# TensorE's slot in another order: output transposes joined with the xn2 transposes, router product next to the h transposes

## The chip, the cores and the metric

The kernel runs on one core of a Trainium2 chip. The metric is the device time of one execution in microseconds (us), lower is better. Engines are called TensorE (PE), VectorE (DVE), ScalarE (ACT), GpSimd (POOL) and SyncE (SP), as the profile's short names have them; PEld is the loading of weights into TensorE.

## The reference

For 32 rows (batch elements) of 512 tokens with 256 channels:

```python
mod = (_silu(L0_c) @ L0_wmod).reshape(32, 6, 1, -1)
sa, ca, ga, sb, cb, gb = ...
h = _layernorm(x, axis=-1) * (1 + ca) + sa
x = x + ga * attn(h)
h = _layernorm(x, axis=-1) * (1 + cb) + sb
x = x + gb * ffn(h)
```

`attn` is a decaying running mean over the tokens (s = a * s + (1 - a) * x_t) times a matrix W, plus a convolution over five tokens per channel. `ffn` has a router: the last token of the row goes through Wp1, gelu and Wp2 to eight logits, and the expert with the largest one is taken for the whole row. The expert is gelu(h W1 + b1) W2 + b2, then Wo, and the result is h + 0.3 * out.

## The kernel before, in words

A row is one unit of work, held whole in the on-chip memory as 128 partitions by 4 tiles of 256 channels (token layout), or as 2 chunks of 128 channels by 512 tokens (channel layout). TensorE changes from one layout to the other by transposes of 128x128, 8 for a row. Products with exact enough results are made from three matmuls each: every operand is split into a high and a low part (`hid_hi`, `hid_lo` and so on), and high x high, low x high and high x low are added up. Setup multiplies W2 and Wo of each expert together, so that only an up product (256 to 512 channels, four groups f = 0 to 3 of six matmuls) and a down product (512 to 256, again four groups of six) are left.

The rows go through a software pipeline with slots i = -3 to 32. In slot i the feed-forward part of row i is computed, row i - 1 is finished and stored, row i + 1 is normalised the second time and routed, row i + 2 goes through mix (W) and convolution, and row i + 3 is normalised the first time and scanned. Each engine has its own list of instructions in program order, written by hand as a function `slot(i)` per engine; they meet only at semaphores. Nothing is scheduled by a tool. TensorE's slot is the subject (`slot`, line 978). Before the change it is in this order:

- `mix(i + 2)` (L915, L916, L919; twelve matmuls, which need S_hi and S_lo of the row)
- the output transposes (`to_tokens(Q, rT, t4_done)`, L967 into the banks Q), after a wait for `oT_ready`
- `up(i, 0)`, `up(i, 1)` (L935 to L937)
- the xn2 transposes ("t3", `to_channels`, L975 into the banks TR)
- `down(i, 0)` (L950, L951 with g_hi, L955 with g_lo), then the first half of `up(i, 2)`
- the router's first product (L1005, four matmul instructions of one column), after waits for `hid_ready` and `gelu_out`
- the second half of `up(i, 2)`
- the h transposes of row i + 3 ("t1", L975 into TR)
- the router's second product (L1017, L1018), after a wait for `nav_ready`
- `down(i, 1)`, `up(i, 3)`, the transposes of the first residual ("t2", L967 into TR), `down(i, 2)`, `down(i, 3)`

ScalarE's slot (L570) is in this order: normalise xn1 (row i + 3) and xn (row i + 1), L507; gelu and g_hi of f = 0 and 1 (L547, L554); hid (L613) and hid_hi (L621) of row i + 1; the router's gelu `nav` (L630), which waits for `r_nav`, the semaphore of the router's first product; `gate1` (L567); gelu 2; h (L643); g_hi 2; S_hi, gelu 3, g_hi 3, S_hi (L541); hid_gated (L679).

GpSimd's slot (L440): the second normalisation's factors; g_lo 0 and 1 (`g_low`, L430, each after a wait for its g_hi); gbeta; hid_lo; the first normalisation's factors (L413 to L418); g_lo 2 and 3; S_lo 0 (L438).

VectorE's slot (L779): rT of row i - 1 (L787); the first `CONV_HEAD` = 4 of ten convolution steps (L748); the two additions of the transposed output to xr (L798), which set `o_ready`; the other steps; statistics (L700); the router's maximum (L829, L831), which sets `sel_ready`; two scans (L776), which wait for h; the first residual with its statistics and S_lo 1 (L764, L755). The banks Q are also where down accumulates, so `down(i, 0)` waits for `o_ready`.

SyncE's queue issues all DMAs of the loop, in program order: the two stores of row i - 1 after `o_ready` (L386), the load of x of row i + 5 into the same buffer once they have landed (L297), and then `fetch(i + 1)` (L362): after `sel_ready` it reads the number of the expert and loads up_w (L375) and down_w (L378). `up(i, 0)` waits for up_w, `down(i, 0)` for down_w.

Of the kernel before, what the change touches and what calls it, by code (L numbers as in the profile page):

```python
# [5 lines left out]
def adaln_attention_ffn_kernel(nc, x, decay_logit, W, b, conv_w, conv_b, Wp1, bp1, Wp2, bp2,  # L6
# [26 lines left out]
    DC = D // P  # L33
# [31 lines left out]
    with ExitStack() as ctx:  # L65
# [6 lines left out]
        def sem(name):  # L72
            return ctx.enter_context(nc.semaphore(name))
# [172 lines left out]
        up_done = sem("up_done")  # L246
# [10 lines left out]

        VECS_LOADED = 16 * 7
        SMALL_LOADED = 16 * 4
        CONV_HEAD = 4  # L260
        CONV_MID = 7
        FIRST = -3

# [7 lines left out]
        def experts_at(i, place):  # L271
            return EXPERTS_AT.get((i, place), ())

        def wait(eng, s, v):
            if v > 0:
                eng.wait_ge(s, v)

        def row(r):
            return 0 <= r < B
# [406 lines left out]
        def _(dve):  # L686
# [55 lines left out]
            def conv(r, first, last):  # L742
                for k, c in CONV_ORDER[first:last]:
                    if k == 0:
                        dve.wait_ge(mix_done, DC * r + c + 1)
                    else:
                        dve.wait_ge(conv_step[c], (TAPS - 1) * r + k)
                    ins = nc.vector.scalar_tensor_tensor(out=Y[c][:, :], in0=h[:, c, k:k + T], scalar=taps[:, c, k:k + 1],  # L748
                                                         in1=Y[c][:, :], op0=ALU.mult, op1=ALU.add)
                    ins.then_inc(conv_step[c] if k < TAPS - 1 else conv_done, 1)  # L750
# [28 lines left out]
            def slot(i):  # L779
# [9 lines left out]
                if row(i + 2):  # L789
                    if i == -2:  # L790
                        dve.wait_ge(s_small, SMALL_LOADED)
                    conv(i + 2, 0, CONV_HEAD)
                if row(i - 1):
# [6 lines left out]
                if row(i + 2):  # L800
                    conv(i + 2, CONV_HEAD, CONV_MID)
                mix_experts = experts_at(i, "mix")
# [41 lines left out]
        def _(pe):  # L844
            mm = nc.tensor.matmul

            def w2_transposes(e):
                pe.wait_ge(s_w2[W2_AT[e]], 16 * nth(W2_AT, e))
                wait(pe, s_w2T, DC * e)
                for c in range(DC):  # L850
                    for f in range(FC):
                        ins = nc.tensor.transpose(U[c][:, f * P:(f + 1) * P], w2_nat(e)[:, f, c * P:(c + 1) * P], ident[:, :])
                ins.then_inc(s_w2T_mm, 1)
# [3 lines left out]
            for c in range(DC):  # L857
                ins = nc.tensor.transpose(U[0][:, c * B:(c + 1) * B], c_nat[:, c * P:(c + 1) * P], ident[0:B, 0:B])
# [5 lines left out]
            for n in range(NMOD):  # L864
                pe.wait_ge(s_wmod[n], 16 * DC)
                for c in range(DC):
                    ins = mm((Y[0], Y[1], Q[0])[n][0:B, :], silu_cT[:, c], wmod_sb[c][n], start=(c == 0), stop=(c == DC - 1))
                ins.then_inc(s_mod_mm, 1)
            w2_transposes(0)
            for m in range(6 * DC):  # L870
                n, at = m * P // 512, m * P % 512
                pe.wait_ge(s_mod_rows, n + 1)
                ins = nc.tensor.transpose(Q[1][:, m * B:(m + 1) * B], mod_rows[n][:, at:at + P], ident[0:B, 0:B])
            ins.then_inc(s_modT, 1)
            pe.wait_ge(s_w, 16)
            for d in range(DC):
                for e in range(DC):
                    ins = nc.tensor.transpose(Y[0][:, d * D + e * P:d * D + (e + 1) * P], w_nat[:, e, d * P:(d + 1) * P], ident[:, :])
# [10 lines left out]
            def expert(e):  # L889
                if e + 1 < E:  # L890
                    w2_transposes(e + 1)
                pe.wait_ge(s_w2T, DC * (e + 1))
                for k in range(2):
                    if e == 0:

                        pe.wait_ge(s_mod_rows, NMOD)
                        pe.wait_ge(s_mods, 1)
                    wait(pe, s_down_lo, 2 * (e - 1) + k + 1 if e else 0)
                    for f in range(FC // 2):
                        fk = k * FC // 2 + f  # L900
                        for c in range(DC):
                            ins = mm(Q[k][:, f * D:(f + 1) * D], w2T(e)[:, c, fk * P:(fk + 1) * P], wo[:, c],
                                     start=(c == 0), stop=(c == DC - 1))
                    ins.then_inc(s_comb, 1)
# [14 lines left out]
                        ins = mm(Y[e][:, :], mix_w[:, 0, d, es], S_lo[:, d], start=False, stop=(d == DC - 1))  # L919
                    ins.then_inc(mix_done, 1)  # L920

            def up(i, f, parts=range(DC)):
                par, n = i % 2, FC * i + f
                if f == 0:
                    pe.wait_ge(up_loaded[par], 16 * (i // 2 + 1))
                    pe.wait_ge(hid_lo_ready, DC * (i + 1))
                if f == 1:
                    wait(pe, sel_ready, i + 1)
                if f == 3:

                    pe.wait_ge(sel_ready, min(i + 2, B))
                wait(pe, gelu_out, n - 1)
                for c in parts:
                    w = c * F + f * P
                    mm(U[f % 2][:, :], up_w[:, par, UP + w:UP + w + P], hid_hi[:, par, c], start=(c == 0), stop=False)  # L935
                    mm(U[f % 2][:, :], up_w[:, par, w:w + P], hid_hi[:, par, c], start=False, stop=False)  # L936
                    ins = mm(U[f % 2][:, :], up_w[:, par, w:w + P], hid_lo[:, par, c], start=False, stop=(c == DC - 1))  # L937
                if DC - 1 in parts:
                    ins.then_inc(up_done, 1)

            def down(i, f):
                par, n = i % 2, FC * i + f
                if f == 0:
                    pe.wait_ge(down_loaded[par], 16 * (i // 2 + 1))

                    wait(pe, o_ready, HB * i)
                pe.wait_ge(g_hi_ready, n + 1)
                for c in range(DC):
                    w = f * D + c * P
                    mm(Q[c][:, :], down_w[:, par, 1, w:w + P], g_hi[:, f], start=(f == 0), stop=False)  # L950
                    mm(Q[c][:, :], down_w[:, par, 0, w:w + P], g_hi[:, f], start=False, stop=False)  # L951
                pe.wait_ge(g_lo_ready, n + 1)
                for c in range(DC):
                    w = f * D + c * P
                    ins = mm(Q[c][:, :], down_w[:, par, 0, w:w + P], g_lo[:, f], start=False, stop=(f == FC - 1))  # L955
                    if f == FC - 1:
                        ins.then_inc(down_done, 1)
                if f < FC - 1:
                    ins.then_inc(down_step, 1)
# [18 lines left out]
            def slot(i):  # L978
                if row(i + 2):
                    mix(i + 2)  # L980
                for e in experts_at(i, "mix"):
                    expert(e)
                if row(i - 1):
                    pe.wait_ge(oT_ready, DC * i)
                    to_tokens(Q, rT, t4_done)
                if row(i):
                    up(i, 0)
                    up(i, 1)
                if row(i + 1):
                    to_channels(i + 1, xn, xn2_ready, t3_done)  # L990
                for e in experts_at(i, "t3"):
                    expert(e)
                if row(i):
                    down(i, 0)
                    up(i, 2, (0,))
                if row(i + 1):
                    r = i + 1
                    if r == 0:
                        pe.wait_ge(s_small, SMALL_LOADED)
                    pe.wait_ge(hid_ready, DC * (r + 1))  # L1000

                    wait(pe, gelu_out, FC * i + 2 if i >= 0 else 0)
                    pe.wait_ge(s_w2T, DC * E)
                    for c in range(DC):
                        ins = mm(U[1][:, 0:1], wp1[:, c], hid_at[r % 2][:, c, T - 1:T], start=(c == 0), stop=(c == DC - 1))  # L1005
                    ins.then_inc(r_nav, 1)
                if row(i):
                    up(i, 2, (1,))
                if row(i + 3):
                    r = i + 3  # L1010
                    to_channels(r, xn1, xn1_ready, t1_done)
                    if r == 0:
                        betas()
                if row(i + 1):
                    r = i + 1
                    pe.wait_ge(nav_ready, r + 1)
                    mm(U[1][0:1, 8:8 + E], nav[:, :], wp2[:, :], start=True, stop=False)  # L1017
                    mm(U[1][0:1, 8:8 + E], ident[0:1, 0:1], bp2_sb[:, :], start=False, stop=True).then_inc(r_logits, 1)  # L1018
                for e in experts_at(i, "t1"):
                    expert(e)  # L1020
                if row(i):
                    down(i, 1)
                    up(i, 3)
                if row(i + 2):
                    r = i + 2

                    pe.wait_ge(h_ready, DC * min(r + 2, B))
                    pe.wait_ge(r1_ready, DC * (r + 1))
                    to_tokens(TR, rT, t2_done)
                if row(i):  # L1030
                    down(i, 2)
                    down(i, 3)
# [31 lines left out]
```

## Time and profile before

| what | value |
|---|---|
| median of 3 runs | 693.33 us (693.09 to 694.68) |
| the profiled execution's own time | 696.09 us |
| its span | 694.1 us |
| TensorE busy | 661.3 us, 95% (3431 matmuls) |
| weight loads busy | 523.1 us, 75% |
| VectorE busy | 570.2 us, 82% |
| ScalarE busy | 570.6 us, 82% |
| GpSimd busy | 459.3 us, 66% |
| granted TensorE clock, mean | 0.974 |

The profile shows one execution. "Busy" is the time in which an engine had an instruction in work; matmuls overlap each other, so that a matmul of 0.39 us may be followed by the next after 0.23 us, and it is the distance of the starts that counts. The granted clock is 1 at 2.4 GHz and 0.5 at 1.2 GHz. Times in a timeline are counted from the start of the span.

### The profile page before, as it was taken

How to read it: one execution, taken by the hardware profiler on the slowest of the kernel's cores; microseconds unless marked ns; L12 is line 12 of the kernel's file. 1: busy time of each engine (PE TensorE's matmuls, PEld its weight loads, DVE VectorE, ACT ScalarE, POOL GpSimd, SP SyncE). 2: the span in 40 equal slices, each digit the busy share in tenths (PEclk: the TensorE clock that was granted, in tenths of full speed). 3: DMA queues.
4: the chain of work that ended last, by engine and by line, in shares of the span. 5: the costliest groups of instructions: out<-in, count | busy, mean ns of one | idle time of the engine just before them, and what ended most of it. 6: DMA issues, size and time to landing. Idle time of an engine off the chain costs nothing.

```text
span 694.1 us, 11042 instructions
## 1 busy us (share of the span) xinstructions
PE 661.3 (95%) x3431; PEld 523.1 (75%) x3431; DVE 570.2 (82%) x870; ACT 570.6 (82%) x979; POOL 459.3 (66%) x528
## 2 busy tenths in 40 slices
PE   5969679999999999999999999999999999999996
PEld 2858557777777878777777777787877778777764
DVE  1677649999999999999999999999999999998711
ACT  3676658888888998888888888899898888887753
POOL 1453537777777777777777777777777777776543
PEclk9798969999999999999999999999999999999998
DMA  7995645555655444555555555545455545544451
GB/s 231 328 301 171 224 153 159 175 171 165 183 182 167 170 131 159 169 179 169 167 181 163 173 181 182 156 149 157 163 167 182 176 160 182 157 148 153 151 170 44
DMA packets 55453, 120.57 MB, mean 174 GB/s; under 512 B 5643, under 2 KB 43364, under 8 KB 46180
## 3 DMA queue, kind: packets, MB, share of 16 engines
q1 hardware_dynamic: 51316, 115.12, 52.7%
q10 hardware_dynamic: 4080, 4.75, 2.5%
q8 instruction: 28, 0.46, 0.3%
q14 instruction: 29, 0.24, 0.1%
HBM read 61.12 MB, written 25.19 MB: 124 GB/s over the span
## 4 chain that ended last, share of the span: by engine, by line
PE 85%; DMA 2%; ACT 2%; POOL 2%; issue 1%; DVE 0%; POOLq 0%; SPq 0%; DVEq 0%; ACTq 0%
PE Q L955 9%; PE Q L950 9%; PE U L935 9%; PE U L937 9%; PE U L936 8%; PE Q L951 8%; PE TR L975 8%; PE Y L919 5%; PE Q L967 4%; PE Y L915 4%; PE Y L916 4%; PE TR L967 4%; PE U L1005 2%; DMA up_table<-up_w 1%; DMA up_w<-up_table 1%
## 5 line engine op out<-in xcount | busy, mean ns | idle before, releaser
L430 POOL TENSOR_TENSOR g_lo<-g,g_hi 128x512 fp32r<-128x512 f32 x128 | 191.3, 1503 | 144.2 <-ACT g_hi L554 138.9
L748 DVE SCALAR_TENSOR_TENSOR Y<-h,taps,Y 128x512 f32<-128x512 f32 x320 | 222.7, 751 | 3.1 <-PE Y L919 0.7
L935 PE MATMUL U<-hid_hi,up_w 128*128 128x512 f32 x256 | 107.1, 418 | 4.7 <-DMA up_w<-up_table 4.7
L950 PE MATMUL Q<-g_hi,down_w 128*128 128x512 f32 x256 | 109.8, 429 | 0.2
L547 ACT ACTIVATE g<-U,up_w 128x512 f32<-128x512 f32 x128 | 88.6, 692 | 25.4 <-PE U L937 22.5
L507 ACT ACTIVATE S<-xr,nmr,rstd 128x256 f32<-128x256 f32 x128 | 66.6, 592 | 48.0 <-POOL S_lo L438 36.4
L937 PE MATMUL U<-hid_lo,up_w 128*128 128x512 f32 x256 | 101.6, 397 | 0.0
L936 PE MATMUL U<-hid_hi,up_w 128*128 128x512 f32 x256 | 101.6, 397 | 0.0
L951 PE MATMUL Q<-g_hi,down_w 128*128 128x512 f32 x256 | 101.1, 395 | 0.0
L776 DVE TENSOR_TENSOR_SCAN S<-keep,h 128x512 f32<-128x512 f32 x64 | 78.0, 1261 | 26.0 <-ACT h L643 26.0
L700 DVE BATCH_NORM_STATS2 st<-xr 128x6 f32<-128x512 f32 x128 | 87.6, 705 | 7.9 <-DMA xr<-in_L_attn_x_dram 3.6
L955 PE MATMUL Q<-g_lo,down_w 128*128 128x512 f32 x256 | 83.7, 408 | 0.7 <-POOL g_lo L430 0.7
L554 ACT CAST g_hi<-g 128x512 fp32r<-128x512 f32 x128 | 80.5, 629 | 3.1
L507 ACT ACTIVATE xn<-xr,nmr,rstd 128x256 f32<-128x256 f32 x128 | 66.5, 591 | 9.5 <-POOL nmr L418 7.2
L416 POOL TENSOR_TENSOR rstd<-rstd,minus_half 128x4 f32<-128x4 f32 x64 | 66.5, 1039 | 0.0
L955 PEld LDWEIGHTS Q<-g_lo,down_w 128*128 128x128 f32 x256 | 45.0, 187 | 23.7 <-POOL g_lo L430 14.4
L787 DVE SCALAR_TENSOR_TENSOR rT<-Q,mods,w_raw 128x512 f32<-128x512 f32 x64 | 44.6, 739 | 18.0 <-PE Q L955 18.0
L935 PEld LDWEIGHTS U<-hid_hi,up_w 128*128 128x128 f32 x256 | 48.8, 191 | 14.1 <-DMA up_w<-up_table 5.4
L937 PEld LDWEIGHTS U<-hid_lo,up_w 128*128 128x128 f32 x256 | 48.6, 190 | 11.4
L438 POOL TENSOR_TENSOR S_lo<-S,S_hi 128x512 fp32r<-128x512 f32 x32 | 54.5, 1704 | 1.9 <-ACT S_hi L541 1.9
L950 PEld LDWEIGHTS Q<-g_hi,down_w 128*128 128x128 f32 x256 | 48.2, 188 | 10.0 <-ACT g_hi L554 0.9
L936 PEld LDWEIGHTS U<-hid_hi,up_w 128*128 128x128 f32 x256 | 49.0, 191 | 8.8
(125 smaller groups left out, 1283.3 us busy)
## 6 DMA issues: line engine op xcount, KB each, us to landing
up_w<-up_table SPq DMA_DIRECT2D x32, 1027.0 KB, 6.6
down_w<-down_tab SPq DMA_DIRECT2D x32, 1024.0 KB, 8.6
xr<-in_L_attn_x_dram SPq DMA_DIRECT2D x32, 512.0 KB, 3.6
out_dram<-xr SPq DMA_DIRECT2D x64, 256.0 KB, 2.3
w_raw<-in_L_ffn_W_dram SPq DMA_DIRECT2D x7, 512.0 KB, 5.2
xr<-in_L_ffn_W_dram ACTq DMA_DIRECT2D x6, 512.0 KB, 7.9
up_table<-down_w SPq DMA_DIRECT2D x2, 1024.0 KB, 7.1
up_table<-up_w SPq DMA_DIRECT2D x2, 1024.0 KB, 6.0
```

Source lines behind the costliest of these rows:

```text
L430: nc.gpsimd.tensor_tensor(g_lo[:, f], g[:, f % 2], g_hi[:, f].bitcast(f32), ALU.subtract).then_inc(g_lo_ready, 1)
L507: nc.scalar.activation(to[:, j], xr[:, r % NX, j], ACT.Identity, bias=nmr[:, j:j + 1], scale=rstd[:, j:j + 1]).then_inc(ready, 1)
L547: nc.scalar.activation(g[:, f % 2], U[f % 2][:, :], ACT.Gelu, bias=up_w[:, i % 2, U_B1 + f:U_B1 + f + 1].bitcast(f32)).then_inc(gelu_out, 1)
L554: nc.scalar.copy(g_hi[:, f], g[:, f % 2]).then_inc(g_hi_ready, 1)
L700: return nc.vector.bn_stats(st[:, k * TPB:(k + 1) * TPB].rearrange("p t s -> p (t s)"), pair)
L748: ins = nc.vector.scalar_tensor_tensor(out=Y[c][:, :], in0=h[:, c, k:k + T], scalar=taps[:, c, k:k + 1], in1=Y[c][:, :], op0=ALU.mult, op1 ...
L935: mm(U[f % 2][:, :], up_w[:, par, UP + w:UP + w + P], hid_hi[:, par, c], start=(c == 0), stop=False)
L936: mm(U[f % 2][:, :], up_w[:, par, w:w + P], hid_hi[:, par, c], start=False, stop=False)
L937: ins = mm(U[f % 2][:, :], up_w[:, par, w:w + P], hid_lo[:, par, c], start=False, stop=(c == DC - 1))
L950: mm(Q[c][:, :], down_w[:, par, 1, w:w + P], g_hi[:, f], start=(f == 0), stop=False)
L951: mm(Q[c][:, :], down_w[:, par, 0, w:w + P], g_hi[:, f], start=False, stop=False)
L955: ins = mm(Q[c][:, :], down_w[:, par, 0, w:w + P], g_lo[:, f], start=False, stop=(f == FC - 1))
```

## The change

TensorE's list is put into another order, and one constant of VectorE's list changes with it.

- The output transposes go from in front of `up(i, 0)` to behind `up(i, 1)`, directly ahead of the xn2 transposes: sixteen transposes in one piece.
- `up(i, 2)` is no longer split. It comes whole, behind the transposes and ahead of `down(i, 0)`.
- The router's first product comes behind `down(i, 0)`, directly ahead of the h transposes.
- `CONV_HEAD` goes from 4 to 6: on VectorE the two output additions come behind six convolution steps.

The lists of ScalarE, GpSimd and SyncE are the same.

```diff
-        CONV_HEAD = 4
+        CONV_HEAD = 6
...
-            def up(i, f, parts=range(DC)):
+            def up(i, f):
...
-                for c in parts:
+                for c in range(DC):
...
-                if DC - 1 in parts:
-                    ins.then_inc(up_done, 1)
+                ins.then_inc(up_done, 1)
...
+                if row(i):
+                    up(i, 0)
+                    up(i, 1)
                 if row(i - 1):
                     pe.wait_ge(oT_ready, DC * i)
                     to_tokens(Q, rT, t4_done)
-                if row(i):
-                    up(i, 0)
-                    up(i, 1)
                 if row(i + 1):
                     to_channels(i + 1, xn, xn2_ready, t3_done)
                 for e in experts_at(i, "t3"):
                     expert(e)
                 if row(i):
+                    up(i, 2)
                     down(i, 0)
-                    up(i, 2, (0,))
                 if row(i + 1):
...
                     ins.then_inc(r_nav, 1)
-                if row(i):
-                    up(i, 2, (1,))
                 if row(i + 3):
                     r = i + 3
                     to_channels(r, xn1, xn1_ready, t1_done)
```

## Rows read from the trace of the kernel before

**Rows 1.** Windows: length, busy us (instructions) of each engine, granted clock, DMA share, GB/s.

```profile
109.00:688.70 579.70, 574.75 (x3028) 454.91 (x3028) 505.19 (x764) 504.32 (x865) 411.65 (x473) 1.00 0.52 164
...
93.60:98.10 4.50, 4.43 (x11) 3.47 (x11) 2.06 (x4) 1.31 (x2) 0.05 (x1) 0.50 0.61 233
```

**Rows 2.** Line 1005, the router's first product: count, ns min/median/max, first and last start.

```profile
L1005 PE MATMUL U<-w_raw,wp x60: 239/250/253, 101.6 to 629.1; 128*128 128x1 f32 x60
...
L1005 PE MATMUL U<-hid,wp x56: 247/250/262, 120.4 to 610.3; 128*128 128x1 f32 x56
```

**Rows 3.** Timeline of TensorE, slot 12: start us, us from first start to last end.

```profile
320.91 1.03 PE L967 MATMUL Q<-ident,rT 128*128 128x128 f32 x8
321.70 0.48 PE L935 MATMUL U<-hid_hi,up_w 128*128 128x512 f32 x1
322.02 0.39 PE L936 MATMUL U<-hid_hi,up_w 128*128 128x512 f32 x1
...
322.94 0.40 PE L937 MATMUL U<-hid_lo,up_w 128*128 128x512 f32 x1
...
327.54 0.58 PE L1005 MATMUL U<-w_raw,wp 128*128 128x1 f32 x4
327.98 0.48 PE L935 MATMUL U<-hid_hi,up_w 128*128 128x512 f32 x1
328.30 0.39 PE L936 MATMUL U<-hid_hi,up_w 128*128 128x512 f32 x1
...
334.44 0.40 PE L951 MATMUL Q<-g_hi,down_w 128*128 128x512 f32 x1
334.83 0.74 PE L955 MATMUL Q<-g_lo,down_w 128*128 128x512 f32 x2
```

**Rows 4.** Timeline of ScalarE, slot 12, and its window 328.38 to 332.41.

```profile
323.37 0.69 ACT L547 ACTIVATE g<-U,up_w 128x512 f32<-128x512 f32 x1 [0.18 <-PE U L937]
...
327.35 1.13 ACT L621 CAST hid_hi<-w_raw 128x512 fp32r<-128x512 f32 x2
328.38 0.26 ACT L630 ACTIVATE nav<-U,vecs 128x1 f32<-128x1 f32 x1
...
328.38:332.41 4.03, 4.03 (x25) 3.19 (x24) 2.76 (x7) 4.03 (x8) 3.79 (x6) 1.00 0.59 147
```

**Rows 5.** Timeline of GpSimd in slot 12, then g_hi 2 and g_lo 2 in slot 28.

```profile
332.56 3.47 POOL L430 TENSOR_TENSOR g_lo<-g,g_hi 128x512 fp32r<-128x512 f32 x2
...
334.74 1.29 POOL L430 TENSOR_TENSOR g_lo<-g,g_hi 128x512 fp32r<-128x512 f32 x1
...
633.01 0.65 ACT L554 CAST g_hi<-g 128x512 fp32r<-128x512 f32 x1
...
633.80 3.46 POOL L430 TENSOR_TENSOR g_lo<-g,g_hi 128x512 fp32r<-128x512 f32 x2 [1.93 <-ACT g_hi L554]
```

**Rows 6.** VectorE's convolution and SyncE's DMA issues in slot 12; the loads' landing times.

```profile
324.28 4.18 DVE L748 SCALAR_TENSOR_TENSOR Y<-h,taps,Y 128x512 f32<-128x512 f32 x6
...
327.34 0.38 SPq L297 DMA_DIRECT2D xr<-in_L_attn_x_dram  x1
331.36 0.37 SPq L375 DMA_DIRECT2D up_w<-up_table  x1
...
DMA to landing us min/median/max: 5.3/6.6/6.9
...
xr<-in_L_attn_x_dram SPq DMA_DIRECT2D x32, 512.0 KB, 3.6
```

**Rows 7.** Timeline of slots 29 and 30: ScalarE, TensorE, SyncE, TensorE.

```profile
648.44 0.26 ACT L630 ACTIVATE nav<-U,vecs 128x1 f32<-128x1 f32 x1
...
648.91 0.20 PE L1017 MATMUL U<-wp,nav 128*1 128x8 f32 x2
...
650.52 0.37 SPq L375 DMA_DIRECT2D up_w<-up_table  x1
...
657.26 1.09 PE L967 MATMUL Q<-ident,rT 128*128 128x128 f32 x8 [1.36 <-DVE rT L787]
```

## The prediction

> **What bounds the kernel now.** The page's first part puts TensorE ahead of all engines, and the windows view says it more sharply: from 109.0 to 688.7 us it is busy 574.75 of 579.7 us at the full granted clock [rows 1]. So the 29 slots from i = 0 to i = 28 follow each other at TensorE's pace; the router product, whose 116 matmuls are four per slot, starts first at 101.6 and last at 629.1 us, hence (629.1 - 101.6) / 28 = 18.84 us a slot [rows 2]. All ordinary slots look alike, so I read one, i = 12, which begins at 317.98 us. In it I looked for what runs beside TensorE without slack, since busy time alone does not show that. Two things stand out. Ahead of the g_lo product of down 2 TensorE waits a little: matmuls come every 0.23 us, but this one comes 0.39 us after the last (334.44 to 334.83) [rows 3]. And ScalarE has no idle time at all from the router's gelu at 328.38 to the end of g_hi 2 at 332.41: 4.03 busy of 4.03 [rows 4]. GpSimd's g_lo 2 starts 0.15 us after that end, at 332.56 [rows 5]. So there is a second chain, as tight as TensorE's own: router gelu, gate, gelu 2, h, g_hi 2 on ScalarE, then g_lo 2 on GpSimd, then down 2 on TensorE. What the page does not say is whether g_lo 2 waits for g_hi 2 or only for GpSimd's previous work, which ends at the same moment. Slot 28 answers: there that previous work is missing, GpSimd idles 1.93 us, and g_lo 2 still starts at 633.80, 0.14 after g_hi 2's end (633.01 + 0.65) [rows 5].
>
> **What the change saves on TensorE.** Eight transposes start 0.11 us apart (1.03 us for eight, 0.27 for the last: 0.76 / 7). The way back to wide matmuls costs 0.03 to the first of them, and that one holds the next off for 0.32 instead of 0.23 (320.91, 321.70, 322.02) [rows 3]. So a return costs 0.03 + 0.09 = 0.12, where one more transpose in the row would cost 0.11: joining the two pieces of eight saves 0.01 us a slot, nearly nothing. The router's four matmuls behind up 2's first half cost 4 x 0.11 and then the same 0.32 for 0.23 (327.98, 328.30) [rows 3]; with transposes behind them that 0.09 goes. Together 0.10 us a slot, or 29 x 0.10 = 2.9 us if TensorE alone decided. The multiplications themselves are the same in number and shape.
>
> **What it moves, in slot 12.** TensorE reaches the end of mix at 320.91 as now [rows 3]. Up 0 and up 1: 12 x 0.232 = 2.78, to 323.69. Sixteen transposes: 15 x 0.109 + 0.03 = 1.67, to 325.36. Up 2 whole: 0.32 + 5 x 0.232 = 1.48, to 326.84. Down 0, with no return in front: 6 x 0.232 = 1.39, to 328.23. The router product starts there instead of at 327.54: 0.69 us later, being behind the second half of up 2. No row shows a router matmul behind a g_lo product; the nearest is the one behind up 2 (0.23 after it), between bounds of 0.03, as after transposes, and 0.39, as at the wait above; I take 0.23.
>
> **What that does to ScalarE.** The router gelu waits for the last of the four. Now that ends at 327.54 + 0.58 = 328.12, and the gelu starts only at 328.38, because ScalarE is busy with hid_hi until 328.48 (two engine instructions overlap by some 0.1) [rows 3, 4]. Afterwards it ends at 328.23 + 0.58 = 328.81. ScalarE starts 0.03 after a matmul's end (322.94 + 0.40 to 323.37) [rows 3, 4], so the gelu starts at 328.84: 0.46 later than now. The work ahead of it even comes earlier: gelu 0 now waits for TensorE until 323.37 with 0.18 idle [rows 4], up 0 will end 0.8 earlier, and so hid_hi ends some 0.17 earlier. That only lengthens ScalarE's idle time before the router's gelu, to about 0.6 us, and what is queued behind it on that engine cannot pass it. Behind it lies the stretch without a gap. So gate, gelu 2, h and g_hi 2 each start 0.46 later, g_lo 2 starts at 333.02, and its reader in down 2 at 334.83 + 0.46 = 335.29. TensorE would have been there at 334.67 - 0.10; it stands 0.7 us, 0.16 of which it stands today. The scan on VectorE, which waits for h, S_lo 0 behind g_lo 3 on GpSimd, and with it mix of the next slot and ScalarE's next normalisation all slip by the same 0.46, so nothing regains it and the next slot repeats it: 18.84 + 0.46 = 19.30 us.
>
> **Bounds of that price.** g_lo 2 and 3 together take 3.47, and g_lo 3 starts at 334.74 and takes 1.29, so g_lo 2 runs for nearly 2.2 [rows 5], while VectorE scans. I take 2.2 again, since the scan slips with h by the same 0.46 and meets it as before. Were it 1.29, g_lo 2 would end before TensorE comes, and the price would be the saving, -0.10 a slot. Upwards the router product's start may be off by 0.16 (the 0.39 above): 0.62 a slot.
>
> **Moves that cost nothing, and their cover.** VectorE's two output additions come behind six convolution steps instead of four. They are over now about when the fifth step starts, 324.28, and six steps take 4.18 [rows 6], so they will be done two steps later, by 325.8; down 0, which needs their bank, starts at 326.84. The router's second product keeps only the eight h transposes between itself and the gelu: that ends at 328.84 + 0.26 = 329.10, TensorE comes at about 329.56. The SP queue: the output stores issue 1.4 later, and the load of x behind them, which waits for their landing, goes from 327.34 to about 328.8, still ahead of the up_w load at 331.36, which lands 5.3 to 6.9 us after its issue [rows 6], so by 338.3; up 0 wants it at 320.91 + 19.30 = 340.2.
>
> **The ends.** Slot 0 has the same router product and the same chain: 29 slots pay. Slot 29 has no h transposes, so the router's second product stands directly behind the first. Now the gelu starts at 648.44 and the product at 648.91, 0.47 later [rows 7]; after the change the gelu is 0.46 later there too and so is the product: another 0.46. In slots 30 and 31 TensorE now stands 1.36 us for the rT of the output transposes [rows 7]. With up 0 and up 1 ahead of them that wait is hidden, but up_w is late next: for slot 30 it is issued at 650.52, that is 1.61 after the router's second product [rows 7], and takes 6.6 [rows 6], so with the shift it lands at 650.52 + 0.46 + 6.6 = 657.6, and up 0, which starts today at 657.26 + 8 x 0.11 = 658.1, gains only 0.5. The half of up 2 ahead of the router product (0.69) takes that back, and the same goes for the up_w load of slot 31. I put slots 29 to 31 at 0 together, between -1.5 and +1.5.
>
> **Sum.** 29 x 0.46 = 13.3. The profiled execution took 696.09 us (span 694.10 and 1.99 around it): 709.4 after. The median of the runs shown is 693.33, 2.76 below the profiled one, and the same 13.3 on it gives 706.6 us.
>
> **Rivals.** (a) **Saved time only, faster.** The delay at the gelu dies out because g_lo 2 takes 1.3 instead of 2.2 once it has left the scan, or the gelu's wait is under 0.06 (it costs nothing as long as the router product starts before 327.6). Then 0.10 a slot is won: 693.33 - 2.9 = 690.4. For it: the present waits of TensorE sum to little; against it: slot 28 and the scan's own dependence on h. 0.05. (b) **They cancel.** g_lo 2 sheds part of its 0.9 excess so that 0 to 0.05 a slot is left: 693 to 695. 0.04. (c) **The x load gets into the up_w load's way.** If up_w landed later by the 3.6 us that the x load takes [rows 6], it would come at 341.9 and up 0 would wait 1.7 a slot on top: 706.6 + 28 x 1.7 = 754. Against it: some 2.5 us between the two issues, and DMA engines busy 52% of the time [rows 1]. 0.02. (d) **The clock.** Thirty-two transposes a slot leave the granted clock at 1.00 all the way from 109.0 to 688.7, at 2.4 GHz; at 0.50 (1.2 GHz), from 93.6 to 98.1, eleven matmuls took 4.5 us [rows 1]. Should sixteen transposes in one piece and a wait of 0.7 bring the lower level for one such stretch a slot, it would cost 4.5 - 11 x 0.232 = 1.9 us in each: 706.6 + 55 = 762. 0.01. The Trainium skill, TensorE: Matmul & The Clock Gate, Part 4: PE-mode transpose, has it that transposes do not bring the clock up as other matmuls do; a piece of 1.7 us in place of two of 0.8 would speak against the change. In this trace full clock holds across pieces of eight, and no run yet shows one of sixteen.
>
> **How the numbers follow.** My forecast has 0.88. The range goes from 701 (g_lo 2 sheds 0.2 a slot: 29 x 0.26, and nothing at the ends, 700.9) to 710 (0.55 a slot and +0.7 at the ends), within the bounds of -0.10 and 0.62. About 0.3%, 2.1 us, is what a measurement of this kernel can tell. Faster by more than that: (a), 0.05. Within: (b), 0.04. Slower: the forecast, (c) and (d), 0.91.
>
> **What would show it.** Slots 19.3 us apart; ScalarE idle about 0.6 before the router's gelu, released by the router product; g_lo 2 still 0.15 behind g_hi 2; TensorE standing some 0.7 in front of down 2's g_lo product; no return after the router product; and the clock at 1.00. I am wrong if the gelu does not wait, if g_lo 2 gets shorter, or if slots come in under 18.9.

## Result and profile after

The changed kernel takes 704.37 us (median of 4 runs, 701.45 to 705.31) against 693.21 of the kernel before: 1.016 times as long, 95% interval 1.014 to 1.018. The forecast was 706.6, in a range of 701 to 710.

The page of the changed kernel, its first and fourth part (busy time; shares of the chain that ended last):

```profile
span 701.6 us, 11042 instructions
...
PE 654.8 (93%) x3431; PEld 524.7 (75%) x3431; DVE 569.8 (81%) x870; ACT 566.8 (81%) x979; POOL 480.5 (68%) x528
...
POOL 32%; ACT 27%; issue 18%; PE 10%; DMA 4%; DVE 2%; POOLq 0%; SPq 0%; ACTq 0%; DVEq 0%
```

TensorE does the same work and is 6.5 us less busy, in a span 7.5 us longer. The chain that ended last, 85% TensorE in the kernel before, now runs mostly over GpSimd and ScalarE. The waits view says where TensorE stands and what ScalarE stands for (us in total, times, longest):

```profile
PEld Q L954 <- POOL g_lo L430: 28.4, 31, 1.0
ACT nav L630 <- PE U L1004: 22.7, 31, 0.8
PE Q L954 <- POOL g_lo L430: 15.0, 31, 0.5
```

The second line is new: 31 times ScalarE stands 0.7 us for the router's first product. The windows view has the clock, and the source view of the router product the pace:

```profile
109.00:690.00 581.00, 563.37 (x2997) 455.08 (x2996) 499.83 (x758) 495.60 (x858) 427.71 (x470) 1.00 0.51 161
```

```profile
L1004 PE MATMUL U<-w_raw,wp x64: 164/250/250, 98.7 to 671.9; 128*128 128x1 f32 x64
```

The granted clock stays at 1.00, as before [rows 1], with TensorE busy 97% instead of 99%. The slots come 19.19 us apart, where they were 18.83.

Slot 12 of the changed kernel begins at 318.69, 0.71 later than in the trace before. TensorE's timeline in it (start us, us from first start to last end):

```profile
321.63 0.40 PE L935 MATMUL U<-hid_hi,up_w 128*128 128x512 f32 x1
...
324.42 1.03 PE L966 MATMUL Q<-ident,rT 128*128 128x128 f32 x8
325.30 1.04 PE L974 MATMUL TR<-ident,xn 128*128 128x128 f32 x8
326.09 0.47 PE L935 MATMUL U<-hid_hi,up_w 128*128 128x512 f32 x1
...
327.56 0.39 PE L949 MATMUL Q<-g_hi,down_w 128*128 128x512 f32 x1
...
328.94 0.50 PE L1004 MATMUL U<-w_raw,wp 128*128 128x1 f32 x4
329.31 1.07 PE L974 MATMUL TR<-ident,S 128*128 128x128 f32 x8
330.31 0.20 PE L1014 MATMUL U<-wp,nav 128*1 128x8 f32 x2
...
335.02 0.39 PE L950 MATMUL Q<-g_hi,down_w 128*128 128x512 f32 x1
335.90 0.72 PE L954 MATMUL Q<-g_lo,down_w 128*128 128x512 f32 x2 [0.50 <-POOL g_lo L430]
```

ScalarE and GpSimd in the same slot:

```profile
323.80 0.67 ACT L547 ACTIVATE g<-U,up_w 128x512 f32<-128x512 f32 x1
...
327.60 1.13 ACT L621 CAST hid_hi<-w_raw 128x512 fp32r<-128x512 f32 x2
329.48 0.26 ACT L630 ACTIVATE nav<-U,vecs 128x1 f32<-128x1 f32 x1 [0.74 <-PE U L1004]
...
332.86 0.65 ACT L554 CAST g_hi<-g 128x512 fp32r<-128x512 f32 x1
```

```profile
332.58 1.07 POOL L418 TENSOR_TENSOR nmr<-nmr,rstd 128x4 f32<-128x4 f32 x1
333.65 3.46 POOL L430 TENSOR_TENSOR g_lo<-g,g_hi 128x512 fp32r<-128x512 f32 x2
...
335.81 1.30 POOL L430 TENSOR_TENSOR g_lo<-g,g_hi 128x512 fp32r<-128x512 f32 x1
```

GpSimd seems not to wait here, since L418, the instruction ahead of g_lo 2, ends at the moment when g_lo 2 starts. In the kernel before the same instruction took a fifth of this:

```profile
332.35 0.21 POOL L418 TENSOR_TENSOR nmr<-nmr,rstd 128x4 f32<-128x4 f32 x1
```

It has the same work in both. In this kernel it starts at 13.9 us of the slot and ends with the start of g_lo 2, so the profile books GpSimd's wait for g_hi 2, some 0.87 us, as this instruction's duration. In run 8 below, where g_hi 2 comes later still, the instruction has its 0.20 again and the wait stands as 1.70 us of idle time. The 21 us by which GpSimd looks busier (480.5 against 459.3 us, 528 instructions each) are mainly this wait, and its share of 32% in the last chain is too high for the same reason.

ScalarE is through with hid_hi at 328.73 and stands until 329.48, when the router product is there. From then on nothing has changed but the time: g_hi 2 ends at 333.51, g_lo 2 starts 0.14 later, its reader on TensorE comes 0.88 after the matmul ahead of it instead of 0.39 [rows 3], and every slot repeats this.

### The profile page after: what moved, and what is told of

It is laid out like the page before. It is cut to its first block, busy times and chain, and to the rows that moved or that the text cites. A ratio compares the mean times of both kernels' runs of the same rounds, so it can differ in the third digit from the quotient of the medians.

```text
span 701.6 us, 11042 instructions
## 1 busy us (share of the span) xinstructions
PE 654.8 (93%) x3431; PEld 524.7 (75%) x3431; DVE 569.8 (81%) x870; ACT 566.8 (81%) x979; POOL 480.5 (68%) x528
## 4 chain that ended last, share of the span: by engine, by line
POOL 32%; ACT 27%; issue 18%; PE 10%; DMA 4%; DVE 2%; POOLq 0%; SPq 0%; ACTq 0%; DVEq 0%
POOL g_lo L430 8%; ACT S L507 7%; POOL hid_lo L462 7%; ACT xn L507 6%; POOL S_lo L438 6%; ACT g L547 5%; POOL rstd L416 4%; POOL nmr L418 4%; DMA up_w<-up_table 3%; ACT hid_hi L621 2%; ACT w_raw L613 2%; ACT hid L613 2%; PE U L935 1%; PE U L937 1%; PE U L936 1%
## 5 line engine op out<-in xcount | busy, mean ns | idle before, releaser
L776 DVE TENSOR_TENSOR_SCAN S<-keep,h 128x512 f32<-128x512 f32 x64 | 76.5, 1237 | 40.2 <-ACT h L643 40.2
L949 PE MATMUL Q<-g_hi,down_w 128*128 128x512 f32 x256 | 107.0, 418 | 0.1
L950 PE MATMUL Q<-g_hi,down_w 128*128 128x512 f32 x256 | 100.9, 394 | 0.0
L949 PEld LDWEIGHTS Q<-g_hi,down_w 128*128 128x128 f32 x256 | 48.1, 188 | 10.7 <-ACT g_hi L554 0.9
```

## Experiments

Four kernels ran first, on one chip beside the kernel before (693.25 us there), then four more (693.02 us). Each ratio is to the kernel before, with its 95% interval. Times of the slot are us from the first matmul of mix, the median over slots 6 to 23 of a kernel's own trace; the distance of the slots is the mean from slot 4 to slot 25.

**1. The router product back inside up 2.** Transposes joined, six convolution steps, the rest as before.

```diff
-                    up(i, 2)
                     down(i, 0)
+                    up(i, 2, (0,))
...
+                if row(i):
+                    up(i, 2, (1,))
```

> The changed kernel with the router's first product put back between the halves of up 2, behind down 0; the sixteen transposes in one piece and the six convolution steps stay. Theory (the loss comes from the router product being late for ScalarE's chain): the product starts at about 9.56 us of the slot, its gelu at 10.1 to 10.2 instead of 10.79, and as up 0 and up 1 now come 0.8 earlier, ScalarE is through with hid_hi at 10.04 and no longer holds the gelu up: the chain is 0.2 to 0.3 ahead of that of the kernel before, slots of 18.55 to 18.6 us, 685 to 687 us in all. Rival A (the sixteen transposes in one piece, or the output additions later, are what costs): slots stay at about 19.2, 703 us. Rival B (TensorE alone decides once the product is back): slots of 18.8, 693 us.

Measured: 699.21 us, ratio 1.008 (1.006 to 1.011), slots of 18.98. Faster than the changed kernel, and a miss of 13 us all the same. TensorE and VectorE in its slot 12 (begins at 318.47) show why:

```profile
325.12 1.04 PE L975 MATMUL TR<-ident,xn 128*128 128x128 f32 x8
326.33 0.47 PE L950 MATMUL Q<-g_hi,down_w 128*128 128x512 f32 x1 [0.17 <-issue]
...
328.49 0.50 PE L1005 MATMUL U<-w_raw,wp 128*128 128x1 f32 x4
```

```profile
324.95 1.28 DVE L798 TENSOR_TENSOR xr<-xr,Q 128x512 f32<-128x512 f32 x2
```

Down 0 needs the banks Q, which VectorE's output additions leave at 326.23. With up 2 behind down 0 nothing covers them, and down 0 starts at 326.33, 0.42 after TensorE was there (the last transpose starts at 325.88, and 0.03 behind it a wide matmul could). So the product is late after all (10.04 in place of 9.56), and its gelu with it (10.58). In the changed kernel up 2 stands there and is the cover: the additions are done at 7.7 of the slot, down 0 starts at 8.9. I had named that cover in the prediction and then took it away in this kernel without counting it.

**2. Only the router product moved.** The kernel before, with up 2 whole ahead of the product.

```diff
                     down(i, 0)
-                    up(i, 2, (0,))
+                    up(i, 2)
...
-                if row(i):
-                    up(i, 2, (1,))
```

> The kernel before with only the router's first product moved behind the whole of up 2; transposes where they were, four convolution steps ahead of the additions. Theory: the product starts 0.69 later, its gelu 0.37 later than before, slots of 19.2 us, 703 to 705 us. Rival A (joined transposes cost): the kernel before's 693 us, or 690 with the return saved.

Measured: 706.38 us, ratio 1.019 (1.015 to 1.023), slots of 19.19, to the hundredth those of the changed kernel. The product's place alone gives the whole loss per slot; the other moves of the change (the joined transposes, up 0 and up 1 ahead of them, the two convolution steps) together add nothing to it and take nothing from it. The time is 1.4 us above what was expected, with runs from 703.10 to 707.93; as the slots agree, that lies outside them or between the runs, and was not looked into.

**3. gate1 ahead of the router's gelu.** The changed kernel, ScalarE's list alone.

```diff
+                if row(i + 2) and i > -2:
+                    gate1(i + 2)
                 if row(i + 1):
                     r = i + 1
                     act.wait_ge(r_nav, r + 1)
                     nc.scalar.activation(nav[:, :], U[1][:, 0:1], ACT.Gelu, bias=vecs[:, V_BP1:V_BP1 + 1]).then_inc(nav_ready, 1)
-                if row(i + 2) and i > -2:
-                    gate1(i + 2)
```

> The changed kernel with ScalarE's gate1 ahead of the router's gelu, so that the 0.7 us in which ScalarE stands for the router product are filled with work that is ready; TensorE's order is the changed one. Theory: gate1 starts at 10.0, its second half waits for the convolution until 10.5, the router's gelu comes at 11.2 and gelu 2 at 11.35 instead of 12.27; g_lo 2 is then held by GpSimd's own work ahead of it, at 14.1 instead of 14.96; slots of 18.35 to 18.45, 680 to 683 us. The router's second product comes at about 11.6 as now, so nothing is lost there. Rival A (the transposes in one piece cost): 695 or more. Rival B (the wait only moves to the router's second product, since its gelu is 0.4 later): slots of 18.8 and more, 693 us.

Measured: 685.46 us, ratio 0.990 (0.987 to 0.992), slots of 18.51: some 19 us less than the changed kernel, with TensorE's order untouched, and faster than the kernel before. ScalarE in this kernel:

```profile
321.59 1.13 ACT L621 CAST hid_hi<-w_raw 128x512 fp32r<-128x512 f32 x2
322.62 1.45 ACT L567 ACTIVATE rT<-Y,mods 128x512 f32<-128x512 f32 x2
323.96 0.27 ACT L632 ACTIVATE nav<-U,vecs 128x1 f32<-128x1 f32 x1
324.10 0.70 ACT L547 ACTIVATE g<-U,up_w 128x512 f32<-128x512 f32 x1
```

No idle time is left between hid_hi and gelu 2. I had expected 680 to 683 us with slots of 18.35 to 18.45; the last 0.1 us was not won. TensorE no longer stands in front of down 2's g_lo product here (it comes 0.23 after the matmul ahead of it), but in mix it stands for S_lo 0, whose product comes 0.39 after the one ahead of it where the kernel before has 0.30:

```profile
331.79 0.40 PE L916 MATMUL Y<-S_hi,mix_w 128*128 128x512 f32 x1
332.18 0.49 PE L919 MATMUL Y<-S_lo,mix_w 128*128 128x512 f32 x1
```

S_lo 0 follows g_lo 3 on GpSimd, which idles 0.11 for g_hi 3 first; that comes from gelu 3, right behind up 3. So the limit has moved to a way over up 3 and no longer goes through gelu 2. How much shorter the slot could be without this wait was not tested.

**4. Four convolution steps again.** The changed kernel with `CONV_HEAD = 4`.

> The changed kernel with four convolution steps ahead of the output additions, as before. Theory: VectorE comes to the additions at 5.1 us of the slot and stands until 6.35 for the transposes, so the steps behind come 1.2 later; gate1's second half waits for the last of them until about 11.75 (0.15 later) and GpSimd's normalisation for the statistics: slots 0.1 to 0.3 longer than 19.2, 706 to 712 us. Rival (the constant is what cost): shorter than 19.2, toward 693 us.

Measured: 708.93 us (2 runs, 706.73 and 711.13), ratio 1.022 (1.018 to 1.027), slots of 19.34. VectorE comes to the additions early and stands for the transposes:

```profile
329.78 1.28 DVE L798 TENSOR_TENSOR xr<-xr,Q 128x512 f32<-128x512 f32 x2 [1.16 <-PE Q L966]
```

The constant is no cost of the change: six steps in place of four save 0.15 a slot in this order of TensorE. The wait of 1.16 on VectorE comes out as 0.15 only, through gate1's second half.

**5. gate1 first in the kernel before.** The edit of 3 on the other kernel.

> The kernel before with ScalarE's gate1 ahead of the router's gelu. Theory: here ScalarE has no idle time in front of the gelu that gate1 could fill; gelu 2 stays at 11.9, the router's gelu comes at 11.7 and the second product at 12.2 instead of 11.76, up 3 and g_lo 3 follow: slots of 18.9 to 19.1, 695 to 701 us. Rival (gate1 first is a gain by itself, whatever TensorE's order): 690 us or less.

Measured: 698.96 us, ratio 1.007 (1.004 to 1.010), slots of 18.96. Here the router's gelu comes 1.44 later, gelu 2 does not come earlier (11.99 against 11.89), and TensorE waits for it ahead of the second product, 32 times, 18.9 us in all by the waits view:

```profile
PEld U L1017 <- ACT nav L632: 18.9, 32, 3.0
```

So the same reordering of ScalarE is worth -19 us behind the new order of TensorE and +6 us behind the old one. The two kernels differ in when ScalarE is through with hid_hi: at 10.13 of the slot in 3, at 10.62 here. Gelu 2 comes 0.48 earlier in 3, which is this difference. It comes with up 0 and up 1 ahead of the transposes and not with the router product's place.

**6. Up 2 split around down 0.** The changed kernel, halves of up 2 ahead of down 0 and behind the router product.

```diff
-                    up(i, 2)
+                    up(i, 2, (0,))
                     down(i, 0)
...
+                if row(i):
+                    up(i, 2, (1,))
```

> The changed kernel with up 2 split again: first half behind the sixteen transposes, then down 0, the router's first product, the second half of up 2, the h transposes. So the output additions stay covered (which they were not in the run with the halves behind down 0, where down 0 stood 0.48 us for them), and the product comes at 9.56 of the slot instead of 10.25. Theory (the product's place is the whole loss, and up 0 and up 1 ahead of the transposes are a gain for ScalarE): the gelu starts at 10.1, 0.3 ahead of the kernel before, g_lo 2 at 14.3, and what bounds then is up 3 with gelu 3, g_lo 3 and S_lo 0 behind it as in the run with gate1 first: slots of 18.5 to 18.6, 684 to 688 us. Rival (something else in the joined order costs): 693 us or more.

Measured: 684.67 us, ratio 0.988 (0.986 to 0.990), slots of 18.56. Both covers hold: half of up 2 hides the output additions, and the product starts at 9.62. ScalarE waits for it by some hundredths:

```profile
321.40 0.62 ACT L621 CAST hid_hi<-w_raw 128x512 fp32r<-128x512 f32 x1
322.09 0.26 ACT L630 ACTIVATE nav<-U,vecs 128x1 f32<-128x1 f32 x1
```

Against the changed kernel this differs by three matmuls' place. Against the kernel before it shows what the joined transposes are good for: with up 0 and up 1 ahead of them ScalarE gets gelu 0 earlier and is through with hid_hi at 10.1 instead of 10.5. The changed kernel has the same gain and wastes it in waiting for the router product.

**7. As 6, with the second half of up 2 behind the h transposes.**

```diff
                     to_channels(r, xn1, xn1_ready, t1_done)
                     if r == 0:
                         betas()
+                if row(i):
+                    up(i, 2, (1,))
```

> As the run before it, but the second half of up 2 behind the h transposes, so that the router product stands next to them (the saved return that the change was to bring) and still comes at 9.56. Theory: TensorE does not decide alone any more, so the return of 0.09 moves little: slots within 0.1 of the run before, 683 to 688 us. Rival (TensorE's returns are what counts): 29 x 0.09 = 2.6 us less than the run before.

Measured: 688.16 us, ratio 0.993 (0.990 to 0.995), slots of 18.65, at the edge of what was expected and 3.5 us more than 6 where the rival had 2.6 less. The product's gelu comes at 10.10, a little earlier than in 6, but gelu 2 now waits for up 2 until 11.74 (11.65 in 6). So the order that saves TensorE a return of 0.09 makes gelu 2 0.09 later, and the slot 0.09 longer.

**8. The product later still.** The changed kernel, its four matmuls behind the h transposes.

> The changed kernel with the four matmuls of the router product behind the h transposes (its waits stay where they are). It starts 0.87 later still, at about 11.1. Theory: the gelu and all behind it start 0.87 later, one to one: slots of 19.19 + 0.87 = 20.05 us, 29 x 0.87 = 25 us more than the changed kernel, 727 to 732 us; the router's second product now waits for the gelu as well. Rival (the delay is partly absorbed): under 720 us.

Measured: 732.49 us (2 runs), ratio 1.057 (1.054 to 1.060), slots of 20.05, as expected to the hundredth. The waits view has ScalarE's wait at 47.3 us in place of 22.7:

```profile
ACT nav L630 <- PE U L1011: 47.3, 31, 1.6
```

The ten kernels side by side, from their traces (start of the router's first product, of its gelu, of gelu 2 and of g_lo 2 with its duration, in us of the slot):

```
                                product  gelu   gelu 2  g_lo 2 (took)  slot   slot - gelu 2
before                           9.57   10.41   11.89   14.59 (2.22)   18.83   6.94
6 up 2 split around down 0       9.62   10.16   11.65   14.33 (2.22)   18.56   6.91
7 as 6, next to h transposes     9.56   10.10   11.74   14.41 (2.21)   18.65   6.91
1 product inside up 2           10.04   10.58   12.06   14.74 (2.21)   18.98   6.92
changed                         10.25   10.79   12.27   14.96 (2.20)   19.19   6.92
2 only the product moved        10.25   10.79   12.28   14.96 (2.20)   19.19   6.91
4 four convolution steps        10.25   10.80   12.46   15.13 (2.20)   19.34   6.88
8 product late                  11.12   11.67   13.15   15.84 (2.20)   20.05   6.90
3 gate1 first                   10.35   11.37   11.51   14.20 (2.21)   18.51   7.00
5 gate1 first, kernel before     9.67   11.85   11.99   14.68 (2.21)   18.96   6.97
```

Whatever was moved, on TensorE, VectorE or ScalarE, the slot is gelu 2's start plus 6.9 to 7.0. In the changed kernel that is g_lo 2 at 14.96, 2.20 for it, 0.05 until TensorE reads it, and 1.97 for the matmuls that are left to the next slot: 19.18. For the six in which gate1 follows the router's gelu and nothing else holds gelu 2 (before, 6, 1, changed, 2, 8) the slot is also the router gelu's start plus 8.38 to 8.42. From the kernel before to run 8, 1.26 us of delay of a 128x1 operation make 1.22 us of slot.

How far this column is a cause shows in what TensorE stands for. Ahead of down 2's g_lo product it stands in six of the ten: the product comes 0.39, 0.35, 0.89, 0.88, 0.96 and 1.22 us after the matmul ahead of it in the kernel before, 7, the changed kernel, 2, 4 and 8, where 0.23 is the distance without a wait. In 1, 3, 5 and 6 it comes after 0.23, and TensorE stands a little for S_lo 0 in mix instead (0.36 to 0.39 in place of 0.30). In 3 and 5 the way that ends last goes over up 3 and not over gelu 2, as said at run 3; in 5 up 3 is itself held up by the router's second product. In 1 and 6 both ways end together within some hundredths, and which one sets the slot is not shown. So the chain over gelu 2 is shown as the cause for the kernel before, the changed kernel and 2, 4, 7 and 8 only.

## Why the prediction was right, point by point

- **What the change saves on TensorE**: as forecast. Sixteen transposes and the return end at 326.09, 4.46 after up 0's start, forecast 4.45; the router product is followed by the transposes with no return. It is worth nothing, as the slot is not TensorE's any more.
- **The router product 0.69 later**: 10.25 against 9.57, as forecast to 0.01. That it stood behind a g_lo product cost nothing extra (0.23), inside the bounds of 0.03 and 0.39.
- **The gelu 0.46 later: the term that was mis-sized, 0.38.** The step that was off is "328.23 + 0.58": I took the four matmuls to last as long as before. They lasted 0.50. In the kernel before the waits for hid are fulfilled only when TensorE gets there, so the weights of the first could not be loaded ahead; the weight loads of both kernels:

```profile
327.51 0.52 PEld L1005 LDWEIGHTS U<-w_raw,wp 128*128 128x128 f32 x4 [0.24 <-ACT w_raw L613]
```

```profile
328.71 0.64 PEld L1004 LDWEIGHTS U<-w_raw,wp 128*128 128x128 f32 x4
```

Before, the load starts 0.03 ahead of its matmul (327.54), in the changed kernel 0.23 ahead (328.94), and the second matmul follows the first after 0.03 instead of 0.11. With the waits long fulfilled, 0.08 is gained back. That makes 0.38 for the gelu; the price per slot was 0.36 instead of 0.46. 29 times the difference is 2.9 us, and the forecast was 2.2 too high. Run 1 separates the wait from the neighbours: there the product stands between the two halves of up 2 as in the kernel before, but `hid` is ready at 327.54 (326.10 + 1.44), long before it, and it has the early load and the 0.50:

```profile
328.26 0.64 PEld L1005 LDWEIGHTS U<-w_raw,wp 128*128 128x128 f32 x4
```

Its matmuls start at 328.49. In the kernel before `hid` is ready at 327.46 (326.02 + 1.44), 0.05 ahead of the load. Run 5, where `hid` is late in the same way, has 0.58 again.
- **ScalarE's idle time**: forecast 0.6, measured 0.74. The forecast had hid_hi end 0.17 earlier, it ended 0.46 earlier (10.04 of the slot against 10.50), as gelu 0, gelu 1 and hid all came earlier, not gelu 0 alone. It only lengthened the wait, as was said.
- **It passes through undiminished**: shown. gate1, gelu 2, h and g_hi 2 each 0.38 later, g_lo 2 0.37, the slot 0.36; and in run 8 with 0.87 more.
- **g_lo 2 keeps its 2.2 us**: it took 2.20 to 2.22 in all ten kernels. Where no scan runs beside it, behind slot 28, it takes 1.3; the kernel before from 640 us on (count, ns min/median/max):

```profile
L430 POOL TENSOR_TENSOR g_lo<-g,g_hi x12: 1284/1292/1304, 644.9 to 685.3; 128x512 fp32r<-128x512 f32 x12
```

That the scan is what stretches it was not tested alone. The Trainium skill, GPSIMD Engine Reference, 1. Specifications, says that GpSimd shares its interfaces to on-chip memory with VectorE, with contention where a VectorE instruction has two inputs there. The scan is such an instruction, and the trace agrees for it. For VectorE's S_lo 1, which has two such inputs as well, it does not: that runs from 336.22 for 1.43 us beside g_lo 3, and g_lo 3 keeps its 1.30.
- **What costs nothing**: the additions' cover held (7.7 against 8.9), and run 1 shows what it is worth, 0.42. The load of x was issued at 329.38, 10.7 of the slot as forecast (328.8 less 317.98 is 10.8), the up_w load 2.56 behind it, and neither held anything up in the 29 slots. The second product had its 0.4 to spare.
- **The ends**: forecast 0, between -1.5 and +1.5. ScalarE's last two router gelus, changed and before:

```profile
655.62 0.26 ACT L630 ACTIVATE nav<-U,vecs 128x1 f32<-128x1 f32 x1 [0.73 <-PE U L1004]
672.22 0.26 ACT L630 ACTIVATE nav<-U,vecs 128x1 f32<-128x1 f32 x1 [0.74 <-PE U L1004]
```

```profile
664.80 0.27 ACT L630 ACTIVATE nav<-U,vecs 128x1 f32<-128x1 f32 x1
```

Slot 29 to 30 takes 16.60 where it took 16.36 [rows 7], and from there to the end of the span it is 29.4 against 29.3. So +0.3.
- **The sum**: the router product of slot 30 in the kernel before:

```profile
663.96 0.58 PE L1005 MATMUL U<-w_raw,wp 128*128 128x1 f32 x4
```

From slot 0's product to slot 30's the changed kernel takes 671.9 - 98.7 = 573.2 us, the kernel before 664.0 - 101.6 = 562.4: 10.8 more. Slot 0's product starts 2.9 earlier in the changed kernel's profiled run (98.7 against 101.6 [rows 2]), although its place in the slot is 0.7 later. That difference lies in setup, where the change does nothing: the profiled execution of the kernel before was itself 2.9 above its median. That is why the sum against that execution (709.4) is farther off than the one against the median (706.6).
- **The rivals**: (a) and (b) needed g_lo 2 to shrink or the gelu not to wait; neither happened. The 327.6 in (a), before which the product was to cost nothing, is too early by the prediction's own figures: the gelu at 328.38 less 0.03 and 0.58 gives 327.77. It changes no chance, as the product came 0.69 later. (c) did not occur. (d) did not either: sixteen transposes in 1.67 us and a stand of 0.65 leave the clock at 1.00. The Trainium skill, TensorE: Matmul & The Clock Gate, Part 4: PE-mode transpose, says that the full clock does not engage for transposes. That would have let one fear a dip; among wide matmuls, pieces of this length bring none.

## What to carry to other kernels

An engine that is 95% busy is not alone in setting the pace: look for a second chain without idle time and for the small operation that it waits on first. Moving a producer by 0.7 us towards its neighbours to save a 0.1 us return delays every in-order consumer behind it; place it by when its consumer is free, or fill the consumer's wait with work that is ready, as gate1 in run 3; where there is no such wait, the same move costs (run 5). And a cover counts for one order only: recount it for each variant, as run 1 shows, since the half of up 2 that hid the output additions was worth 0.42 a slot. And the time of an instruction can hold a wait of the next one, as GpSimd's L418 here: compare its duration with that in a kernel where nothing is late.

## What was unexpected

- A group of four one-column matmuls takes 0.50 instead of 0.58 when its waits are fulfilled before TensorE gets there (second start after 0.03 instead of 0.11).
- Run 2's later product (+13 us) and run 5's gate1 first (+6 us) each lose alone, yet gate1 first in the changed kernel wins 8 us over the kernel before. The third part is up 0 and up 1 ahead of the transposes, which alone with the product in its old place wins as much (run 6). A later product with gate1 first, but without that, was not run. The fastest kernel is run 6, 684.67 us, 1.2% below the kernel before.
- ScalarE starts gelu 0 0.30 earlier in the slot than before: in ordinary slots it no longer waits for TensorE there, and starts it while its last normalisation is still ending (323.80, with that one ending at 323.90).
- GpSimd's wait of 0.87 us does not appear as idle time but as the duration of the instruction ahead of it.
